# One layer of gated cross-attention and retrieved experts, on one core: the gather matmuls split in two, one for each half of the partitions

## What is computed

```python
de = down_embed[indices]                        # b t h k d
ue = up_embed[indices]
z = jnp.einsum('btd,bthkd->bthk', h, de)        # one number for each slot
z = act(z * jax.nn.softmax(sc, axis=-1))
out = jnp.einsum('bthk,bthkd->btd', z, ue)
```

## Time and profile before

| | us |
|---|---|
| median of 3 runs | 1285.93 (1282.44 to 1288.79) |
| the profiled execution, its own time | 1286.89 |
| its span in the profile | 1285.1 |
| TensorE matmuls busy | 1181.4 (92%) |
| TensorE weight loads busy | 1042.7 (81%) |
| VectorE busy | 1122.3 (87%) |
| ScalarE busy | 638.4 (50%) |
| GpSimd busy | 331.0 (26%) |

### The profile page before, as it was taken

One profiled execution on the slowest core, in us unless ns is written; L12 is line 12 of the kernel. 1 busy time (PEld: TensorE's weight loads), 2 busy tenths in 40 slices (PEclk: granted clock), 3 DMA queues, 4 the chain that ended last, 5 costly groups with the idle time before them and its releaser, 6 DMA issues.

```text
span 1285.1 us, 47501 instructions
## 1 busy us (share of the span) xinstructions
PE 1181.4 (92%) x19324; PEld 1042.7 (81%) x19324; DVE 1122.3 (87%) x4298; ACT 638.4 (50%) x1834; POOL 331.0 (26%) x152
## 2 busy tenths in 40 slices
PE   5676999999999999999999999999999999999866
PEld 3665888888888888888888888888888888888755
DVE  1457899999999999999999999999999999999963
ACT  3254465555545655555456555554565555545310
POOL 1223122333331223333311233332122333331110
PEclk9887999999999999999999999999999999999878
DMA  7005345554544465455444554554445545543562
GB/s 200 6 6 122 106 120 143 143 108 112 142 119 114 121 143 143 100 121 142 122 111 121 143 143 98 122 142 111 117 125 143 141 105 117 142 119 109 129 148 51
DMA packets 300320, 153.33 MB, mean 119 GB/s; under 512 B 278111, under 2 KB 291271, under 8 KB 291911
## 3 DMA queue, kind: packets, MB, share of 16 engines
q1 hardware_dynamic: 300103, 150.29, 47.3%
HBM read 78.44 MB, written 4.72 MB: 65 GB/s over the span
## 4 chain that ended last, share of the span: by engine, by line
PE 86%; DVE 6%; issue 5%; ACT 2%; POOL 1%; DMA 0%; SPq 0%; POOLq 0%; DVEq 0%; ACTq 0%
PE bank L989 16%; PE bank L833 12%; PE bank L820 11%; PE bank L870 9%; PE bank L843 8%; PE bank L939 5%; PE bank L878 3%; PE bank L910 3%; PE bank L858 3%; PE bank L920 3%; PE bank L889 2%; PE bank L976 2%; PE bank L907 2%; PE bank L956 1%; PE bank L853 1%
## 5 line engine op out<-in xcount | busy, mean ns | idle before, releaser
L989 PE MATMUL bank<-ue,coef 128*128 128x256 f32 x1024 | 226.5, 379 | 1.1 <-ACT coef L403 1.1
L340 POOL TENSOR_TENSOR rstd<-veps,minus_half 128x1 f32<-128x1 f32 x32 | 17.6, 551 | 783.4 <-DVE veps L736 783.4
L989 PEld LDWEIGHTS bank<-ue,coef 128*128 128x128 f32 x1024 | 192.1, 190 | 26.2 <-ACT coef L403 1.4
L833 PE MATMUL bank<-uc,hot_r 128*128 128x32 bf16 x6144 | 161.0, 177 | 32.8 <-issue 32.8
L833 PEld LDWEIGHTS bank<-uc,hot_r 128*128 128x128 bf16 x6144 | 157.5, 96 | 38.9 <-issue 38.8
L820 PEld LDWEIGHTS bank<-z,hot_rT 128*128 128x128 bf16 x2048 | 155.3, 96 | 29.3 <-issue 28.9
L820 PE MATMUL bank<-z,hot_rT 128*128 128x32 bf16 x2048 | 161.7, 177 | 7.4 <-DVE picked L571 5.9
L820 PE MATMUL bank<-zl,hot_rT 128*128 128x32 bf16 x2048 | 160.9, 177 | 0.0
L820 PE MATMUL bank<-zll,hot_rT 128*128 128x32 bf16 x2048 | 160.8, 177 | 0.0
L820 PEld LDWEIGHTS bank<-zl,hot_rT 128*128 128x128 bf16 x2048 | 155.9, 96 | 0.0
L820 PEld LDWEIGHTS bank<-zll,hot_rT 128*128 128x128 bf16 x2048 | 155.6, 96 | 0.0
(11 more groups left out here) (140 smaller groups left out, 2238.6 us busy)
## 6 DMA issues: line engine op xcount, KB each, us to landing
hot_rT<-expert_rows SPq DMA_DIRECT2D x64, 1024.0 KB, 6.4
xt<-in_x SPq DMA_DIRECT2D x32, 128.0 KB, 2.5
out<-x1k SPq DMA_DIRECT2D x32, 128.0 KB, 2.1
ue<-in_L_ffn_up_embed SPq DMA_DIRECT2D x1, 2048.0 KB, 17.1
ct<-in_ctx SPq DMA_DIRECT2D x32, 32.0 KB, 2.2
z<-in_L_ffn_W_up SPq DMA_DIRECT2D x1, 1024.0 KB, 8.5
expert_rows<-r_h SPq DMA_DIRECT2D x64, 8.0 KB, 1.8
hot_r<-hot_rT SPq DMA_TRANSPOSE x64, 7.0
```

The costliest lines, as they stand in the source:

```text
L833: last = mm(bG[k % 2][:, 32 * (q - 16 * k):32 * (q - 16 * k) + 32], hot_r[:, q, :], uc[:, n, q, :], start=(n == 0), stop=(n == 2))
L989: last = mm(bG0[:, 0:DM], coef[:, c, :, :].rearrange("r h q -> r (h q)"), ue[:, c, :], start=(c == 0), stop=(c == C - 1))
```

## The change

Each gather matmul becomes two: for h = 0 and 1, the 64 weight columns of half h, moving the 16 columns of the token of that half, with the result in partitions 64 h to 64 h + 63. Only the wanted blocks are computed. A pair then takes 16 columns of a bank instead of 32, so gather(0) and gather(1) share bank2, gather(2) and gather(3) bank3, and no gather waits for VectorE any more. `gathered` and `gathered_sum` are called twice instead of four times, over all 128 partitions and 512 columns; picked is twice as large. gathered(0) now waits for gather(1), and stands behind the score maxima. scatter(0) and scatter(1) wait for gm0 and gm1.

```diff
@@ -137,7 +137,7 @@
-        picked = sb("picked", [128, 2, 16, C])
+        picked = sb("picked", [128, 2, 32, C])
...
@@ -560,22 +560,15 @@
                 cs = 1 - side
 
                 def gathered(k):
-                    Ct.wait(f"g_pe{k}")
+                    Ct.wait(f"g_pe{2 * k + 1}")
                     Ct.wait("hotc")
-                    if k < 2:
-                        Ct.free(f"zs{k + 2}")
-                    else:
-                        Ct.wait(f"zs{k - 2}")
-                    for half in range(2):
-                        rows = slice(64 * half, 64 * half + 64)
-                        last = nc.vector.tensor_tensor(picked[rows, k % 2, :, :],
-                                                       bG[k % 2][rows, :].rearrange("s (q h c) -> s q h c", q=16, h=2)[:, :, half, :],
-                                                       hot_c[rows, 16 * k:16 * k + 16, :], ALU.mult)
-                    last.then_inc(S[f"gm{k}"], 1)
+                    Ct.free(f"zs{k}")
+                    nc.vector.tensor_tensor(picked[:, k, :, :], bG[k][:, :].rearrange("s (q c) -> s q c", q=32),
+                                            hot_c[:, 32 * k:32 * k + 32, :], ALU.mult).then_inc(S[f"gm{k}"], 1)
 
                 def gathered_sum(k):
                     Ct.wait(f"gm{k}")
-                    nc.vector.tensor_reduce(zs[:, 16 * k:16 * k + 16], picked[:, k % 2, :, :], AX.X, ALU.add).then_inc(S[f"zs{k}"], 1)
+                    nc.vector.tensor_reduce(zs[:, 32 * k:32 * k + 32], picked[:, k, :, :], AX.X, ALU.add).then_inc(S[f"zs{k}"], 1)
 
                 def hot_T(part):
 
@@ -654,22 +647,17 @@
                     nc.vector.tensor_copy(r_h[:, :], rc_i[:, 0, :]).then_inc(S["rh_ok"], 1)
                 if Fw:
                     up_silu(0)
-                if Ct:
-                    gathered(0)
                 if Fw:
                     up_silu(1)
                 if A:
                     scores_max(0)
                     scores_max(1)
                 if Ct:
+                    gathered(0)
+                    gathered_sum(0)
                     gathered(1)
-                    gathered_sum(0)
                     gathered_sum(1)
-                    gathered(2)
-                    gathered(3)
-                    gathered_sum(2)
-                    gathered_sum(3)
-                    Ct.wait("zs3")
+                    Ct.wait("zs1")
                     nc.vector.tensor_tensor(zp[:, :], zs[:, :], p_sm[:, cs, :], ALU.mult).then_inc(S["zp_ok"], 1)
                 if Ct:
 
@@ -812,13 +800,12 @@
                     if k == 0:
                         Ct.wait("zll_ok")
                         Ct.free("y_ok")
-                    if k >= 2:
-                        Ct.wait(f"gm{k - 2}")
                     parts = [zz[:, cs, :, :].bitcast(H)[:, :, 1::2] for zz in (z, zl)] + [zll[:, cs, :, :]]
                     for q in range(16 * k, 16 * k + 16):
                         for n, part in enumerate(parts):
-                            last = mm(bG[k % 2][:, 32 * (q - 16 * k):32 * (q - 16 * k) + 32], hot_rT[:, q, :],
-                                      part.rearrange("r (h q) c -> r h q c", h=2)[:, :, q, :], start=(n == 0), stop=(n == 2))
+                            for h in range(2):
+                                last = mm(bG[k // 2][64 * h:64 * h + 64, 16 * (q % 32):16 * (q % 32) + 16], hot_rT[:, q, 64 * h:64 * h + 64],
+                                          part[:, Q * h + q, :], start=(n == 0), stop=(n == 2))
                     last.then_inc(S[f"g_pe{k}"], 1)
 
                 def scatter(k):
@@ -827,7 +814,7 @@
                         for n in range(3):
                             Ct.wait(f"uc{n}")
                     Ct.wait_dma(f"hotr_in{k // 2}")
-                    Ct.wait(f"gm{k + 2}" if k < 2 else f"w_sb{k - 2}")
+                    Ct.wait(f"gm{k}" if k < 2 else f"w_sb{k - 2}")
                     for q in range(16 * k, 16 * k + 16):
                         for n in range(3):
                             last = mm(bG[k % 2][:, 32 * (q - 16 * k):32 * (q - 16 * k) + 32], hot_r[:, q, :], uc[:, n, q, :],
```

More of the change, by code:

```diff
@@ L181, in flamingo_layer @@
             "e_ok rci_ok rh_ok rdup_ok dif_ok ex_ok exs_ok exr_ok p_ok sm_pe sm_ok rows_out "
-            "rows_in0 rows_in1 hotrT0 hotrT1 hotr_in0 hotr_in1 hotc g_pe0 g_pe1 g_pe2 g_pe3 gm0 gm1 gm2 gm3 zs0 zs1 zs2 zs3 zp_ok zt_ok u_ok uh1 uh2 uh3 ul_ok "
+            "rows_in0 rows_in1 hotrT0 hotrT1 hotr_in0 hotr_in1 hotc g_pe0 g_pe1 g_pe2 g_pe3 gm0 gm1 zs0 zs1 zp_ok zt_ok u_ok uh1 uh2 uh3 ul_ok "
             "uc0 uc1 uc2 w_pe0 w_pe1 w_pe2 w_pe3 w_sb0 w_sb1 w_sb2 w_sb3 out_pe y_ok y_out0 y_out1"
```

## The result

The changed kernel took 1442.97 us (median of 4 runs, 1439.93 to 1445.23); the kernel before, on the same chip, 1284.83 (4 runs). The ratio is 1.1224, with a 95% interval of 1.1191 to 1.1257. Slower was forecast, and the time lies within the range of 1310 to 1452, but the likeliest case (1381) fell short by 62 us. The time is that of rival 3: the supply of instructions and a fall of the clock on top (1445). One execution of all, one of e12_zt, took 1785 us at a mean granted clock of 0.57, and is left out of that kernel's time.

A forecast was written before the change was run, and what follows sets the result against it. TensorE was taken to bound the steady turn, with instruction supply limiting the changed gather. 29 turns x 3.1 = 90 us plus 5 for the run-out, on 1286.9, gave 1382, less 1.0 for the median: 1381 us; range 1310 to 1452.

The forecast's parts named there:

- the likeliest case: Whole kernel: instruction supply limits the gather while the clock stays whole; 1381 us, chance 0.60.
- rival 3: Work behind the gather: new stops drop the clock to 1.2 GHz, +2 us per turn on top, 1445 us; chance 0.11.
- Supply of instructions: TensorE's gather: instructions come in blocks of 256, one per 3.5 us, too slow for the split; +3.1 us per turn.
- The stretch: First gather matmul to L889 in a turn: 9.6 us instead of 6.47.
- the change of form: TensorE passing between tile forms: two new passes per turn, 0.1 us each, hidden behind slow instruction supply.
- just one block is fetched ahead: TensorE's instruction queue: the next block is asked for only when one is entered, and takes 3.5 us.
- broadcasts of expert rows hold up a packet: DMA: 1 MB broadcasts delay instruction packets on their way, but are issued only when the gathers are done.
- The array: Gather matmuls on TensorE: halves overlap, 29 ns per pair (25.8 to 32), +0.56 us per tile, hidden by supply.
- The clock: Steady part: granted clock stays at 1.00, adding nothing to the likeliest sum.
- signs of being wrong: Profile after: gather without stops, a falling clock, or a turn not near 39.7 us.
- VectorE as nothing: Products and sums in the steady turn: 2.2 us per tile freed on VectorE, counted as no gain.
- Run-out: Last three tiles: longer gathers against a dropped 5.9 us wait and less VectorE work; +5 us together.

The follow-up runs named there:

- e12_zt: Kernel before with dense(3) ahead of scatter(0) and, on ScalarE, tanh(zt) ahead of hT; 1289.19 us, ratio 1.0036.
- e1: Changed kernel with only the first half (h = 0) of each gather pair computed; 1393.75 us.
- e4: Kernel before with 16 moving columns instead of 32 in each gather matmul, 128 weight columns kept; 1310.13 us.
- e2: Changed kernel with all matmuls of half 0 of a gather, then all of half 1, instead of alternating; 1746.24 us.
- e3: Kernel before with each gather matmul split into two halves of 64 weight columns, both moving all 32 columns, VectorE's work unchanged; 1426.65 us.
- e7: Kernel before with two of the three bf16 parts of z, so two thirds of the gather matmuls; 1303.56 us.
- e8: Changed kernel with VectorE's products and sums in the old sizes, in their new places; 1450.01 us, ratio 1.1305.
- e5: Changed kernel with two of the three bf16 parts of z, so two thirds of the gather's instructions; 1312.55 us.
- e10: Kernel before with dense(3) ahead of scatter(0) and hot_c on VectorE moved ahead of the silu; 1289.83 us, ratio 1.0033.

## Why the prediction was right or wrong

**Supply of instructions: right, in mechanism and size.** The stretch was to be 9.6 us and is 9.61; about 200 packets were to come and 202 came; a stop put down to "issue" stands in the gather of each turn, and none in the kernels with half the instructions (e1, e4) or a slow pace (e2). The packets in the gather of the second turn, in 40 slices of 0.25 us from 634 to 644 us:

```profile
GB/s 6 27 0 0 0 0 66 0 0 0 0 0 0 0 0 0 0 0 0 0 0 66 0 0 0 0 0 0 0 98 393 33 66 426 459 459 459 393 360 492
```

The two lone ones are in slices 6 and 21 (counted from 0), 3.75 us apart, as in the earlier trace rows. Two things more bear it out. The added packets fit to the unit: 48 for 12288 added instructions, 256 each. And the stops end with the packets: each of the 26 stops of over 0.9 us in turns 4 to 28 ends 1.2 to 1.5 us after a packet of queue 8 has landed (in e3 25 stops, 1.2 to 1.6), and the next packet starts at least 1.0 us after that. One point was told wrongly: stops of about 1.5 us, two in a turn (its own sum, 9.6 less 7.2 us for the array, the scores and the change of form, leaves 2.4 for both). In turns 4 to 28 there is one of over 0.9 us in each, and a second in a single turn; the longest is 2.0 us. I put it down to this, that the block in which the 1.6 us of scores fall lasts nearly as long as the next takes to come, and that the array is slower than I took it. Neither changes the stretch, which the blocks set: what the array needs more is taken from the stops, as the prediction had it. Another slip is in its sum: +2.9 and +3.5 us per turn give 1375 and 1392 us, not 1366 and 1398. That just one block is fetched ahead remains a reading of the spacing and of these times; no run changed the fetch itself. And that broadcasts of expert rows hold up a packet, as the prediction says, the packets' own times don't show: in the kernel before, 25 packets beside heavy transfers took 0.93 us (median), the 105 without any 1.13.

**The array: right.** A pair at 31.3 ns in the mean of a gather, where I took 29 between 25.8 and 32. The halves overlap (e2). The load of 64 columns lasts longer than the old one of 128, as this row of the changed kernel's loads in order of time shows beside the 96 ns of the earlier trace rows:

```profile
632.26 0.12 PEld L807 LDWEIGHTS bank<-z,hot_rT 128*64 128x64 bf16 x2
```

So the split halves the columns and loses the fast kind of load: two halves together need more time than the whole did. The Trainium skill, TensorEngine Tiling (Array Packing), Restrictions, says that column tiling disables Fast Weight Load; the trace agrees, with 31.7 ns for each load of one half with its matmul (e1) against 25.0 for a whole one. The floor of about 25 ns from start to start that the Trainium skill gives in TensorE: Matmul & The Clock Gate, Back-to-back issue gap, holds here over the full array (25.0, with 32 moved columns and with 16), but not between the two halves: there two matmuls start 3 ns apart, and the measurement decides.

**The clock: the step that failed.** The likeliest case kept 1.00 in the steady part and put the clock at nothing in its sum, and the fall had a chance of 0.11; it measured 0.94. Two of the prediction's own signs of being wrong came: the clock fell, and the turn is 41.88 us in the mean, not near 39.7. Its mechanism and its price were on paper and came true: L926 takes 2.96 to 3.57 us (3.26 was said), L876 1.05 for 0.48, 1.9 us a turn (2 was said), and 1445 us in all. The chance was wrong, for two reasons. I set the new stops of 1.6 us against one standstill of 3 us in the run-out, and took the shorter ones as probably harmless; e7 shows falls, in 17 of 25 turns, behind stops of 1.2 us a turn. And I didn't ask at all what a gather of half the moving columns does to the clock; e4 shows that this alone lets it fall, in 15 of 25 turns, with no stop and not one instruction more. How the 5.19 us divide between the two stays open. A turn grew by 5.23 us instead of 3.1, and 29 x 2.1 = 62 us is what the likeliest case lacks; 1.9 of the 2.1 us lie behind the gather, at the low clock.

**VectorE as nothing: nearly right.** It is worth 0.5 to 0.7% (e8), little of it in the steady turn, where it was counted as 0. Its sum was right: 65 us less busy for 70.

**Run-out and start-up.** +5 us was taken for the run-out with the dropped wait; what follows the 29 turns takes 12.2 us more. The gathers stop there too, with more than before between them. From the chain of its last turns:

```profile
1374.01 2.36 PE bank L807 x139
1376.37 2.70 issue
1379.07 3.58 PE bank L807 x128
...
1383.09 3.29 PE bank L807 x117
```

A stop of 2.70 us is longer than any in turns 4 to 28, and behind it 128 and 117 matmuls take 28 ns each, where 139 took 17 ahead of it; the granted clock is 1.00 ahead of the stop and 0.50 behind it. Which of the two, stop or clock, makes up the missing 7 us I didn't separate. The start-up gave 6.0 us back. Its length differs between all these kernels (first gather matmul at 124.6 to 132.4 us), without a relation to the edit that I can show; this stays open.

## What to carry to other kernels

Before splitting a matmul into smaller ones, count the instructions: here TensorE is fed 256 per 3.4 to 3.75 us, about 14 ns each. A gather of 804 at about 8 ns stopped in every turn and one of 548 in 16 of 25 (e5), however well the pieces overlap in the array; one of 420 at 12.5 ns (before, e4) didn't. The columns that a product throws away may be what keeps the clock up, so price the work behind a phase at both levels of the clock when the phase becomes thinner or gets gaps. And an idle gap in a pipeline of two engines that wait for each other in turn is not a gain in hand: look first at what is late next.

## What the runs showed of the hardware that was not expected

- A gather of the same length, with the same instructions and no stop, but 16 columns moved instead of 32, is followed by the lower clock in 15 of 25 turns (e4: 0.97 in the steady part, 1.00 before).
- Matmuls to alternate column halves come in pairs, 3 ns apart within a pair and 31.7 ns from pair to pair; to one half they start 31.7 ns apart (e1, e2), whole ones 25.0 ns.
- Each stop of over 0.9 us in the gather ends 1.2 to 1.5 us after a packet of 16 KB in queue 8 has landed.
- Passing from the new form to the next costs about 0.1 us at each place: 108 ns from gather to causal matmul and 131 ns to L876, where it was 25.
- A two-input operation of VectorE over 64 columns takes 1787 ns instead of 273 while GpSimd works on two large inputs (e10), and hot_c 2200 instead of 680.
